# Attention stage: low-key products on half the rows for two query tiles together, a turned tile between, the bias table in four pieces, half of each share added on VectorE

## What is computed

```python
q, k = _rope(q, c, s), _rope(k, c, s)               # 4 batches, 16 heads, 1024 x 64
scores = jnp.einsum('bhqd,bhkd->bhqk', q, k) * SCALE
kb = -p * jnp.log1p(a * dist)                       # per head, by distance |i - j|
attn = jax.nn.softmax(scores + kb[None], axis=-1)
out = jnp.einsum('bhqk,bhkd->bhqd', attn, v)
return out.transpose(0, 2, 1, 3).reshape(Bb, Ss, H * D) @ out_w.T
```

## Time and profile before

| what | value |
|---|---|
| median of 3 runs | 1968.41 us (1962.46 to 1969.35) |
| profiled execution | 1962.84 us, span 1961.1 us, granted clock 0.971 |
| attention stage in the trace | from about 497 to 1690 us |
| PE / DVE / ACT / POOL busy over the span | 92% / 76% / 59% / 75% |
| time between two heads' shares | 17.27 us, 17.77 us or, where a table is loaded, 20 to 22 us |

### The profile page before, as it was taken

One profiled execution on the slowest core, in us unless ns is written; L12 is line 12 of the kernel. 1 busy time (PEld: TensorE's weight loads), 2 busy tenths in 40 slices (PEclk: granted clock), 3 DMA queues, 4 the chain that ended last, 5 costly groups with the idle time before them and its releaser, 6 DMA issues. The chain is left out here.

```text
span 1961.1 us, 39818 instructions
## 1 busy us (share of the span) xinstructions
PE 1809.5 (92%) x12356; PEld 1048.2 (53%) x12356; DVE 1496.1 (76%) x2828; ACT 1163.7 (59%) x1724; POOL 1472.4 (75%) x871
## 2 busy tenths in 40 slices
PE   4999899998699999999999999999999999599988
PEld 3655633333355555555555555555555555256656
DVE  5244589999688788788788788788888788698841
ACT  6553422222677777777677777677777777322133
POOL 5250067778699899899899899899899899555421
PEclk8999999999799999999999999999999999799989
DMA  4254335464598988888888888888888988500001
GB/s 153 90 190 152 84 114 165 155 212 169 137 179 176 197 183 177 194 183 178 193 183 173 188 185 178 190 183 176 194 184 181 200 184 176 123 0 1 1 6 38
DMA packets 714150, 295.28 MB, mean 151 GB/s; under 512 B 619264, under 2 KB 678658, under 8 KB 714064
## 3 DMA queue, kind: packets, MB, share of 16 engines
q1 hardware_dynamic: 674784, 245.23, 56.8%
q10 hardware_dynamic: 37248, 46.14, 6.7%
q0 software_dynamic: 2048, 3.15, 0.6%
HBM read 102.39 MB, written 58.85 MB: 82 GB/s over the span
## 5 line engine op out<-in xcount | busy, mean ns | idle before, releaser
L1223 POOL TENSOR_TENSOR probs_lo<-probs 128x1024 bf16<-128x1024 f32 x512 | 958.1, 1900 | 80.4 <-DMA probs_t_lo<-probs_lo 54.4
L1191 ACT ACTIVATE probs<-scores,neg_max 128x1024 f32<-128x1024 f32 x512 | 588.7, 1150 | 266.2 <-DVE neg_max L1117 231.6
L1117 DVE CUSTOM_DVE_ANT_0 scores<-score_ps,bias_tab 128x1024 f32<-128x1024 f32 x512 | 624.9, 1221 | 120.1 <-issue 113.9
L1040 PE MATMUL score_ps<-k_hi_hi,q_hi_lo 128*128 128x512 bf16 x1024 | 392.8, 384 | 24.6 <-DVE ident_bf L1177 18.1
L1041 PE MATMUL score_ps<-k_lo_lo,q_hi_lo 128*128 128x512 bf16 x1024 | 391.1, 382 | 0.0
L1049 PEld LDWEIGHTS turn_ps<-ident_bf,probs 128*128 128x128 bf16 x4096 | 273.4, 99 | 146.7 <-issue 26.8
L1049 PE MATMUL turn_ps<-ident_bf,probs 128*128 128x128 bf16 x4096 | 316.0, 221 | 20.7 <-ACT probs L1191 20.7
L1068 PE MATMUL pv_ps<-probs_t_hi,v_hi_lo 128*128 128x512 bf16 x1024 | 262.9, 380 | 11.0 <-DVE share L1157 7.6
L1198 ACT COPY probs_t_hi<-turn_ps 128x1024 bf16<-128x1024 bf16 x256 | 255.8, 999 | 20.0 <-PE turn_ps L1049 16.1
L887 PE MATMUL proj_ps<-xn_t,wqk 128*128 128x512 f32 x512 | 232.7, 608 | 7.9 <-DVE rotated L777 5.9
L791 POOL TENSOR_TENSOR qk_parts<-rotated,qk_parts 128x1024 bf16<-128x1024 f32 x64 | 135.9, 2125 | 125.0 <-ACT qk_parts L785 124.7
(11 more groups left out here) (225 smaller groups left out, 2378.4 us busy)
## 6 DMA issues: line engine op xcount, KB each, us to landing
qk_parts<-qk_parts ACTq DMA_DIRECT2D x64, 512.0 KB, 3.4
q_hi_lo<-qk_parts SPq DMA_DIRECT2D x128, 128.0 KB, 2.8
k_hi_hi<-qk_parts SPq DMA_DIRECT2D x128, 128.0 KB, 2.9
k_lo_lo<-qk_parts SPq DMA_DIRECT2D x128, 128.0 KB, 2.9
v_hi_lo<-v_parts SPq DMA_DIRECT2D x64, 256.0 KB, 3.2
bias_tab<-bias_by_distance SPq DMA_DIRECT2D x16, 960.0 KB, 6.6
probs_t_lo<-probs_lo SPq DMA_TRANSPOSE x512, 3.3
v_parts<-cos_tables ACTq DMA_DIRECT2D x12, 512.0 KB, 2.7
```

What stands on the lines that cost most here:

```text
L1040: pe.matmul(o[:, cs[c]], QS[s][:, q], KS[s][:, cs[c]], start=True, stop=False)
L1117: v.tensor_tensor_reduce(SB[n % 2][:], sp_[n % 2][:], TB[s][:, j:j + S], -1.0, 3.0e38, ALU.add, ALU.min, neg_max[:, n % 16:n % 16 + 1]).th ...
L1191: act.activation(PR[n % NP][:], SB[n % 2][:], ACT.Exp, bias=neg_max[:, m:m + 1], scale=-1.0, accum_out=row_sum[:, m:m + 1]).then_inc(exped, 1)
L1223: g.tensor_tensor(LQ[n % NL][:], PR[n % NP][:], PRB[n % NP], ALU.subtract).then_inc(low_made, 1)
```

## The change

- `low_keys`: the low-key product uses only q's high part. `QX` is a second copy of it on rows 64 to 127; the left 512 columns are made on rows 0 to 63, the right 512 on rows 64 to 127. So each of the four products of two tiles has 64 rows instead of 128, and the product of the two low parts is left out.
- PE makes the scores of two tiles in one (even) step, u+14 and u+15: high keys of the first, a turn, high keys of the second, then the low keys of both. `s_ready` of both tiles comes only there. DVE, ACT run one tile further ahead of the turn (`LS`, `LE` one more).
- The table is loaded in four pieces of 240 KB, one behind each of four transposes. The q and k loads stand behind tiles 6 and 14, and there are seven.
- The second half of a share is scaled and added by four DVE instructions of 128 columns straight from PSUM; POOL adds only the first half. The reciprocal stands one step earlier.

```diff
-    sp.dma_start(K.KL[s][0:DH, :], q[rows, 3, :]).then_inc(K.qk_in[s], DMA)
-    sp.dma_start(K.KL[s][DH:P, :], q[rows, 3, :]).then_inc(K.qk_in[s], DMA)
+    sp.dma_start(K.QX[s][DH:P, :], q[rows, 0, :]).then_inc(K.qk_in[s], DMA)
+    for c in range(2):
+        cols = slice(c * CH, c * CH + CH)
+        sp.dma_start(K.KL[s][c * DH:c * DH + DH, cols], q[rows, 3, cols]).then_inc(K.qk_in[s], DMA)
-def load_table(sp, K, g, s):
+def load_table(sp, K, g, s, k):
+    n = TAB // 4
+    tab = bass.AP(tensor=K.fscr.tensor, offset=(g * 2 + s) * FLEN + k * n, ap=[[1, P], [1, n]])
+    sp.dma_start(K.TB[s][:, k * n:k * n + n], tab).then_inc(K.tab_in[s], DMA)
...
-    LS, LE, LT = LV + 11, LV + 10, LV + 9
+    LS, LE, LT = LV + 12, LV + 11, LV + 9
+        LOADS = (BT - 2, U - 2)
...
-                    if n in (BT, U - 1) and not (last and b == B - 1):
+                    if n in LOADS and not (last and b == B - 1):
...
+                    if LOADS[0] < n <= LOADS[0] + 4 and b == B - 1 and not last:
+                        load_table(sp, K, g + 1, 0, n - LOADS[0] - 1)
+                    k = (n - LOADS[1] - 1) % U
+                    if k < 4 and n > LOADS[1] and b == B - 1 and not last:
+                        load_table(sp, K, g + 1, 1, k)
+                    elif k < 4 and n < BT and b == 0 and not (isinstance(it, int) and it == 0):
+                        load_table(sp, K, g, 1, k)
...
+                for cs in halves:
+                    pe.matmul(sp_[n % 2][:, cs], QS[s][:, q], KS[s][:, cs], start=True, stop=False)
+            def low_keys(n):
+                s = n // BT % 2
+                for i in range(2):
+                    q = slice((n + i) % BT * P, (n + i) % BT * P + P)
+                    for c, cs in enumerate(halves):
+                        rows = slice(c * DH, c * DH + DH)
+                        mm = pe.matmul(sp_[i][:, cs], (QS, QX)[c][s][rows, q], KL[s][rows, cs], start=False, stop=True)
+                    mm.then_inc(s_ready, 1)
...
-                if there(u + LS):
+                pair = there(u + LS) and (u + LS) % 2 == 0
+                if pair:
                     scores(it, u + LS)
                 if there(u + LT):
                     turn(it, u + LT)
+                if pair:
+                    scores(it, u + LS + 1)
+                    low_keys(u + LS)
...
+                v.tensor_tensor(SH[:], ov[0][:], last_axis(inv[:, BT * h:BT * h + 4], D), ALU.mult).then_inc(scaled, 1)
...
+                for k in range(4):
...
+                    ins = v.scalar_tensor_tensor(out=acc, in0=ov[1][:, k, :], scalar=inv[:, BT * h + 4 + k:BT * h + 5 + k],
+                                                 in1=acc, op0=ALU.mult, op1=ALU.add)
+                ins.then_inc(scaled, 1)
...
-                if there(n) and j == V_STEPS - 1:
+                if there(n) and j == HI_STEPS:
                     invert(it, hh)
```

More of the change, by code:

```diff
@@ L898, in load_scores_in @@
     sp.dma_start(K.KS[s][DH:P, :], q[rows, 2, :]).then_inc(K.qk_in[s], DMA)
-    sp.dma_start(K.KL[s][0:DH, :], q[rows, 3, :]).then_inc(K.qk_in[s], DMA)
-    sp.dma_start(K.KL[s][DH:P, :], q[rows, 3, :]).then_inc(K.qk_in[s], DMA)
-def load_table(sp, K, g, s):
-    tab = bass.AP(tensor=K.fscr.tensor, offset=(g * 2 + s) * FLEN, ap=[[1, P], [1, TAB]])
-    sp.dma_start(K.TB[s][:], tab).then_inc(K.tab_in[s], DMA)
+    sp.dma_start(K.QX[s][DH:P, :], q[rows, 0, :]).then_inc(K.qk_in[s], DMA)
[6 more added lines that the diff above has]
+    sp.dma_start(K.TB[s][:, k * n:k * n + n], tab).then_inc(K.tab_in[s], DMA)
 def attend(nc, K, io, sb, ps, sem):
@@ L940, in attend @@
     OL = [sb(f"out_t_lo{i}", [P, CH], BF16) for i in range(2)]
-    SH = [sb(f"share{i}", [P, 4, D]) for i in range(2)]
+    SH = sb("share", [P, 4, D])
     ot_hi, wo_ready = [sem(f"ot_hi{c}") for c in range(2)], sem("wo_ready")
@@ L1030, in _ @@
         def _(pe):
+            halves = [slice(c * CH, c * CH + CH) for c in range(2)]
             def scores(it, n):
-                s, t, k = n // BT % 2, n % BT, n // U
-                if t == 0:
-                    pe.wait_ge(qk_in[s], at(it, 6 * DMA, 6 * DMA * (k + 1)))
+                s, k = n // BT % 2, n // U
+                if n % BT == 0:
+                    pe.wait_ge(qk_in[s], at(it, 7 * DMA, 7 * DMA * (k + 1)))
                 if not (isinstance(it, int) and it == 0 and n < 2):
                     pe.wait_ge(biased, at(it, U, n - 1))
-                o, q = sp_[n % 2], slice(t * P, t * P + P)
-                cs = [slice(c * CH, c * CH + CH) for c in range(2)]
-                for c in range(2):
-                    pe.matmul(o[:, cs[c]], QS[s][:, q], KS[s][:, cs[c]], start=True, stop=False)
-                    mm = pe.matmul(o[:, cs[c]], QS[s][:, q], KL[s][:, cs[c]], start=False, stop=True)
-                mm.then_inc(s_ready, 1)
+                q = slice(n % BT * P, n % BT * P + P)
+                for cs in halves:
[8 more added lines that the diff above has]
+                    mm.then_inc(s_ready, 1)
             def turn(it, n):
@@ L1111, in bias_max @@
                 if t == 0:
-                    v.wait_ge(tab_in[s], (it + n // U) // B * DMA + DMA)
+                    v.wait_ge(tab_in[s], (it + n // U) // B * (4 * DMA) + 4 * DMA)
                 if not (isinstance(it, int) and it == 0 and n < 2):
@@ L1153, in scale_share @@
                 v.wait_ge(recip, at(it, 2, hh + 1))
-                for c in range(2):
-                    v.wait_ge(op_ready, at(it, 4, 2 * hh + c + 1))
-                    v.wait_ge(added, at(it, 4, 2 * hh + c + 1))
-                    v.tensor_tensor(SH[c][:], ov[c][:], last_axis(inv[:, BT * h + 4 * c:BT * h + 4 * c + 4], D),
-                                    ALU.mult).then_inc(scaled, 1)
+                v.wait_ge(op_ready, at(it, 4, 2 * hh + 1))
+                v.wait_ge(added, at(it, 2, hh + 1))
+                v.tensor_tensor(SH[:], ov[0][:], last_axis(inv[:, BT * h:BT * h + 4], D), ALU.mult).then_inc(scaled, 1)
+                v.wait_ge(op_ready, at(it, 4, 2 * hh + 2))
+                v.wait_ge(scaled, at(it, 4, 2 * hh + 2))
+                for k in range(4):
+                    row = (it % B) * BT + 4 + k
+                    acc = K.SACC[:, row, :] if isinstance(row, int) else K.SACC[:, bass.ds(row, 1), :].rearrange("p o d -> p (o d)")
+                    ins = v.scalar_tensor_tensor(out=acc, in0=ov[1][:, k, :], scalar=inv[:, BT * h + 4 + k:BT * h + 5 + k],
+                                                 in1=acc, op0=ALU.mult, op1=ALU.add)
+                ins.then_inc(scaled, 1)
             def step(it, u, there):
@@ L1223, in low, with add_share @@
                 g.tensor_tensor(LQ[n % NL][:], PR[n % NP][:], PRB[n % NP], ALU.subtract).then_inc(low_made, 1)
-            def add_share(it, h, c):
-                g.wait_ge(scaled, at(it, 4, 2 * h + c + 3))
+            def add_share(it, h):
+                g.wait_ge(scaled, at(it, 4, 2 * h + 3))
                 g.sem_inc(add_begun, 1)
-                row = (it % B) * BT + 4 * c
+                row = (it % B) * BT
                 acc = K.SACC[:, row:row + 4, :] if isinstance(row, int) else K.SACC[:, bass.ds(row, 4), :]
-                g.tensor_tensor(acc, acc, SH[c][:], ALU.add).then_inc(added, 1)
+                g.tensor_tensor(acc, acc, SH[:], ALU.add).then_inc(added, 1)
             def step(it, u, there):
@@ L1235, in step @@
                     low(it, u + LT)
-                for c in range(2):
-                    if there(u) and u % BT == BT - 2 + c:
-                        add_share(it, u // BT, c)
+                if there(u) and u % BT == BT - 2:
+                    add_share(it, u // BT)
             g.wait_ge(zeroed, 1)
-            g.nop().then_inc(added, 2)
+            g.nop().then_inc(added, 1)
             run(g, step)
@@ L1704, in program @@
             K.QS = [sb_in(f"q_hi_lo{s}", [P, S], BF16) for s in range(2)]
+            K.QX = [sb_in(f"q_hi_again{s}", [P, S], BF16) for s in range(2)]
             K.KS = [sb_in(f"k_hi_hi{s}", [P, S], BF16) for s in range(2)]
```

8 lines of the change are left out of this document (3 added, 5 removed).

## The result

| | before | changed |
|---|---|---|
| median, 4 runs each | 1966.32 us (1962.46 to 1969.35) | 2009.8 us (2005.54 to 2018.64) |
| profiled execution | 1962.84 us, span 1961.1 | 2018.64 us, span 2016.7 |
| ratio | 1 | 1.0228 [1.0183, 1.0273] |

The account below looks back on a forecast made before the run. The prediction took the PE, DVE, ACT loop (17.77 us a head) as the bound, not POOL alone. Loop 61 x (18.0 - 18.33) = -20 us, tables +10, start +1, together -9 to -12, gave about 1957 us; range 1920 to 2000.

Parts of the forecast that it names:

- loop, a head: Attention stage: a chain of score pairs through PE, DVE and ACT takes 18.0 us a head, against 18.33 before with tables.
- pairs 1 to 4: A head's four score pairs, by PE's work with v: high parts 4.1 us, low parts 4.47, take-out 4.93, share 4.55.
- four short instructions: DVE's four 128-column instructions for half the share: 4 x 0.267 = 1.07 us, costing 0.5 us a head.
- row halves, a change of tiling: PE's low-key products: two 64-row halves run side by side, and each change of tiling costs 0.10 us.
- tables, all: Loading the tables in pieces: 14 times 0 to 35 us in all, taken as 0.7 us each, 10 us.
- start: Start of the attention stage: one tile more of lead before the first turn, +1 us.
- the whole table keeps the queue still for 5.9 us: SP's issues behind a table before the change: 5.9 us of silence, used as upper bound for a piece's landing time.
- a piece comes just in time or up to 2.5 us late: DVE's need for the table: last piece issued at 14.2 us, landing at 17 to 18, wanted at 17.6.
- late pieces: Rival, table loads: SP stands still 1.5 us behind each piece, DVE waits some 3 us 14 times; 1989 us, chance 0.20.
- Row halves one after the other: Rival, PE's low keys: the halves don't overlap, each pair takes 0.43 us more on PE; 1996 us, chance 0.20.
- detours that vanish: Rival, DVE: take-out and share fit in its gaps, so a head takes 16.8 us; 1885 us, chance 0.12.
- POOL's waits: Sign in POOL's timeline: gaps of nearly 2 us a head, with waits on ACT and no longer on the transposes.

Follow-up runs that it names:

- e2: Changed kernel with a table's four pieces issued directly behind one another and the tables loaded only once, for all heads: ratio 0.9922 to the kernel before.
- e5: Changed kernel with SP's loop over the six middle groups written out: ratio 1.0117 to the kernel before.
- e7: Changed kernel with a table's four pieces issued at once and SP's loop written out: ratio 1.0008 to the kernel before.
- e18: e7 with the q and k loads spread over several transposes: ratio 0.9953 to the kernel before.
- e20: e18 with SP's loop made a loop again: ratio 1.0129 to the kernel before.
- e1: Changed kernel with a table's four pieces issued directly behind one another: ratio 1.0177 to the kernel before.
- e19: Kernel before with SP's loop written out, the table whole in one DMA, loads earlier and spread: ratio 0.9842 to the kernel before.
- e14: Kernel before with SP's loop written out, the table's four pieces at once, loads earlier and spread: ratio 0.9841 to the kernel before.

## Why the prediction was wrong

| term of the sum | predicted | found |
|---|---|---|
| loop, a head | 18.0 us | 18.12 us |
| pairs 1 to 4 | 4.1, 4.47, 4.93, 4.55 | 4.15, 4.48, 4.95, 4.55 |
| four short instructions | 1.07 us, 0.5 a head | 1.04 us, 0.43 a head |
| row halves, a change of tiling | together, 0.10 | together, 0.10 |
| tables, all | 10 us | 58 us |
| start | +1 us | +4.0 us |
| sum over the stage | -9 to -12 us | +49 us |

The measured pairs are from first low-key product to first low-key product, as means of the two heads from 1030.31 to 1066.55 us (4.17, 4.48, 5.10, 4.55 and 4.12, 4.48, 4.79, 4.55). The loop was right in its mechanism and by 0.12 us a head too short, which is 7 us: 0.05 of it is the prediction's own rounding of 18.05 to 18.0, and no pair is off by more than 0.05 in the mean. The pair of the take-out is 0.17 us above the prediction in one head and 0.14 below it in the next. Why heads alternate by 0.64 us was not settled; e2, where DVE's wait for the table needs no arithmetic on registers, has 0.33. What makes the start 4.0 us longer is open too.

The step that failed is "the whole table keeps the queue still for 5.9 us", and with it "a piece comes just in time or up to 2.5 us late". It cost 48 us. The sum of the 61 periods in the traces takes the 57.9 us of the tables apart: with SP's loop written out (e5) 30.1 are left above 61 x 18.12, with the pieces at once as well (e7) 9.5, with the loads spread too (e18) none. The mistake has three sides.

- *The silence was put down to the table.* It belongs to the jump of SP's loop. The trace of before held the disproof twice: a table of the same size with a transpose 0.61 us behind it, and heads with the second table that take 21.93 to 22.23 us at the five pairs inside SP's loop, but 20.39 and 19.73 at the first and the last pair, outside it. The prediction read one second table alone. So I counted the silence as removed, and it stayed: e5 takes 22 us off by writing the loop out, e20 against e18 35.
- *The wish for the table was dated too late.* SP's times came out as predicted: from the transpose ahead of the loads to the last piece 14.2 us (796.98 - 784.14 + 1.4). But a piece took 3.8 us to land, the last one up to 5.0, and DVE wanted it 16 us after the low part of tile 6, not 17.6: it waits 3.3 us beyond its usual 1.0. At the second table the jump comes on top, between first and second piece, and it is 7.4 (6.2 to 7.4 at the five jumps, 2.3 and 3.3 at the pairs outside). In the kernel before, the table was out at once behind the loads, and no wait of DVE at a pair with tables is over 2.2 us: the wait for pieces is new.
- *The slack was counted as cover, not as recovery.* Before, POOL's floor of 17.27 under a loop of 17.77 gave back 0.5 us a head behind each pair. The changed loop is held by DVE and PE, which a late table delays too: behind a pair its heads take 18.44 and 17.80 at once, and nothing comes back. Where only transposes are late and no table is (e7), the head behind a pair takes 17.05 and something does.

Of the rivals, late pieces (1989 us) had the place right, DVE behind a table wait, and the cause wrong: SP doesn't stand still behind a piece, and the second table waits more than twice the 3 us I gave it. Row halves one after the other and detours that vanish are both refuted, by the start times and by 18.12. Of the signs that the prediction named, the period, the low-key products and the four instructions came; POOL's waits did not (125 us on DVE's share and 54 on transposes against 29 on ACT), nor did a wait of at most 1 us for the table (3.3 to 8.4 us, 14 times). The range ended too low because I bounded the pieces from the same misread silence.

What the change was worth part by part, then: half height with the pair order wins something and costs more (half height -18 us, the half share on DVE 0.43 us a head or +26 away from tables, the loop as a whole +20; the other 12 or so, an estimate by subtraction, are the order in pairs, which no run took alone). The pieces between transposes cost 21 us by e7 against e5 (10 by e1 against the changed kernel, within the intervals), and the silence was there before and is no longer paid back.

## What to carry to other kernels

When a wait is put down to an operation, look at every place where the same operation stands: if one of two has no wait, something else ends there, such as the body of a loop. An engine that only issues DMAs can stand still at a loop's jump, as SP did here; the jump belongs where nothing waits for its next DMA, or the loop is written out. Before moving a cost to an engine with slack, ask whether that slack was what repaid the stalls; and an order of instructions that wins in one schedule (the cast first) can lose in another, so it is tried in the one in which it will stand.

## What the runs showed of the hardware

- SP's jump back over a body of 64 transposes and their loads: with tables under way 3.4 to 3.7 us of silence in the changed kernel (3.7 from 811.96 to 815.67), 3.8 to 4.3 in e20, 5.2 to 5.4 in the kernel before, five jumps each; 3.4 us without tables (e2). In e20 the DMA engines ran empty in it.
- Two matmuls of 64 rows on the two halves of the array start within 0.01 us of each other, and a pair takes the 0.22 us of one.
- A table of 960 KB in one DMA or in four of 240 KB cost the same (e19, e14): nothing, where it went out ahead of the loads and these were spread over the transposes behind it.
